# Moving the low halves of the second layer's experts from GpSimd to VectorE, one hidden unit late, in a fused two-layer language-model tower

## The chip, the cores and the metric

The kernel runs on one core of a Trainium2 chip. The metric is the device time of one launch in microseconds (us), the median of several runs. The engines are TensorE (PE, with its weight loads as PEld), VectorE (DVE), ScalarE (ACT), GpSimd (POOL) and SyncE (SP, which issues the DMAs).

## What is computed

4096 tokens (16 rows of 256) pass through two layers of width 256. Cut to what matters here:

```
h = embed(x)
h = h + rwkv_block(layernorm(h))               # layer 0, time and channel mix
h = h + dense_moe(layernorm(h))                # layer 0: 8 experts, hidden 1024, gelu, top-2 gates
h = h + rwkv(layernorm(h))                     # layer 1
x = h; x = x + attention(rms(x))               # layer 1: 16 heads of 16, causal, 256 keys
o0 = gelu(xf @ e0_up.T) @ e0_down.T            # layer 1: four experts on xf = rms(x)
o1 = silu(xf @ e1_w1.T) * (xf @ e1_w2.T) @ e1_down.T
o2 = gelu(gelu(gelu(xf @ e2_l1.T) @ e2_l2.T) @ e2_l3.T) @ e2_l4.T
o3 = gelu(gelu(xf @ e3_down.T) @ e3_up.T) @ e3_out.T
moe = wts0 * o0 + wts1 * o1 + wts2 * o2 + wts3 * o3
```

All products are made from bf16 pairs: a number is kept as a high half (it, rounded to bf16) and a low half (it minus the high half, rounded to bf16), and TensorE adds three products, high by high, high by low and low by high.

## The kernel before, in words

The tokens are cut into 8 tiles of TT = 512. A first phase (to about 457 us) embeds them and runs layer 0's RWKV block. The second phase, `phase_bc`, does the rest, in stages, and each stage works on three tiles at once: the 8 dense experts of layer 0 on tile i, layer 1's RWKV and attention (the `front`) on tile i - 1, and layer 1's four experts on tile i - 2.

**Units.** The work of the experts is cut into units. `U` is an up product of a dense expert with its gelu, `D` the down product of one. `I` is an up product of a second-layer expert with its gelu, `G` the gated one (silu times a product), `O` a down product. `U`, `I` and `G` are the hidden units: each makes one 128 x 512 block of hidden values. A stage has 64 hidden units of the dense experts; a tile of the second layer's experts has 26 (22 `I`, 4 `G`), so 208 for all 8 tiles.

**A hidden unit.** PE fills one of two PSUM banks (`c_up`). ACT takes the gelu into one of four f32 buffers `g` (line 1580) and writes the high half (line 1582); for a `G`, DVE makes the gated value in two steps (`gated`, lines 1934 and 1938) and ACT the high half (line 1572). Then the low half is `g` minus the high half, a `tensor_tensor` of 128 x 512: on DVE for the dense experts (line 1955), on POOL for the second layer's (line 1418). ACT's gelu of hidden unit h waits for the low half of h - 4, since the buffers go round. PE's down products wait for both halves.

**The order.** Nothing is scheduled at run time. Each engine walks the same list of tokens: the front's steps (`f0`, `r2`, `Rb0`, `A1`, `f5d`, `g5`, ...) and, braided between them by fixed weights, the units. Each engine does at a token what is its own there, and waits on semaphores in that order. So an instruction that waits holds up everything behind it on its engine. On POOL the second layer's low halves stand in the same queue as the reciprocal square roots of the norms (lines 1357 to 1380), the low halves of the front's inputs (1386, 1404) and two of every three heads' low halves of the attention weights (1396; DVE does the third at 1851, and the high halves at 1848; ACT the exponentials at 1535). On DVE the dense low half of unit n is already one unit late: it is done at the token of unit n + 1.

**The stages.** One with dense units alone, one with dense units and front, five full ones (`ORDER_BC`, period 313.7 us), one without second-layer units, then `ORDER_CC` (2744 to 3011 us: no dense units, the last front, two tiles of second-layer experts with 52 hidden units) and `PLAN_C` (3011 to 3084 us: the last tile's 26).

Of the kernel before, what the change touches and what calls it, by code (L numbers as in the profile page):

```python
# [8 lines left out]
ALU = mybir.AluOpType  # L9
# [4 lines left out]
BATCH, SEQ, D = 16, 256, 256  # L14
# [779 lines left out]
LAG = 3  # L794
# [97 lines left out]
class Plan:  # L892
# [47 lines left out]
    def braid(self, order):  # L940
# [13 lines left out]
        return tokens + self.units[n:]  # L954

    def last_use(self, piece):

        if piece[0] == "B":
            return self.units.index(("D", 4 * piece[1] + 3))
        users = [n for n, u in enumerate(self.units) if u[0] in "IGO"  # L960
                 and c_piece("e1_w1" if u[0] == "G" else u[1], u[-2]) == piece]
        return users[-1]
# [40 lines left out]
def phase_bc(nc, c, out):  # L1003
# [5 lines left out]
    with ExitStack() as x:  # L1009
# [121 lines left out]
        up_ps = Both(x.enter_context(nc.semaphore("c_up_ps")), NB, len(PLAN_C.bank_user))  # L1131
        hi_ready = Both(x.enter_context(nc.semaphore("c_hi_ready")), NB, len(PLAN_C.hid))
        lo_dense = Both(x.enter_context(nc.semaphore("c_lo_dense")), NB, 0)
        lo_expert = Both(x.enter_context(nc.semaphore("c_lo_expert")), 0, len(PLAN_C.hid))

        def low_half(i, plan, h):

            unit = [u for u in plan.units if u in plan.hid][h]
            if unit[0] == "U":
                return lo_dense.sem, lo_dense.at(i, unit[1] + 1)  # L1140
            return lo_expert.sem, lo_expert.at(i, sum(u[0] != "U" for u in plan.hid if plan.hid[u] <= h))
        g_ready = Both(x.enter_context(nc.semaphore("c_g_ready")), NB, len(PLAN_C.gelu))
# [42 lines left out]
        def slot_of(plan, u):  # L1185

            if u[0] == "U":
                return 8 + u[1] % 6
            return plan.home["e1" if u[0] == "G" else u[1], u[-1]] + u[-2]
# [161 lines left out]
        def _(pool):  # L1351
# [60 lines left out]

            def dense(i, plan, before):
                def step(u):
                    if u[0] in "IG":
                        h, a = plan.hid[u], slot_of(plan, u)
                        pool.wait_ge(hi_ready.sem, hi_ready.at(i, h + 1))
                        pool.tensor_tensor(lo14[:, a, :], g[:, h % 4, :], hi14[:, a, :],  # L1418
                                           ALU.subtract).then_inc(lo_expert.sem, 1)
                return tokens_of(i, plan, step)  # L1420
            run(pool, lambda: None, {}, dense, front, lambda t: {})

        @block.scalar
        def _(act):
# [138 lines left out]
            def dense(i, plan, before):  # L1563
                def step(u):
# [9 lines left out]
                    if h >= 4:  # L1574
                        act.wait_ge(*low_half(i, plan, h - 4))
                    elif before is not None:
                        act.wait_ge(lo_dense.sem, lo_dense.at(i))
                        act.wait_ge(lo_expert.sem, lo_expert.at(i))
                    bias = c.b1[:, u[1]:u[1] + 1] if u[0] == "U" else 0.0
# [13 lines left out]
        def _(dve):  # L1593
# [336 lines left out]
            def dense(i, plan, before):  # L1930
                def gated(u):
                    n, h = plan.up[u], plan.hid[u]
                    dve.wait_ge(gate_th.sem, gate_th.at(first_tile(i), plan.gate[u] + 1))
                    E.done(dve.scalar_tensor_tensor(sl[:, :], sl[:, :], 1.0, ub[n % 2][:, :], ALU.add, ALU.mult))
                    E.settle()
                    dve.wait_ge(up_ps.sem, up_ps.at(i, n + 2))
                    dve.wait_ge(*low_half(i, plan, h - 4))
                    dve.scalar_tensor_tensor(g[:, h % 4, :], sl[:, :], 0.5, ub[(n + 1) % 2][:, :], ALU.mult,
                                             ALU.mult).then_inc(gate_sl.sem, 1)
# [11 lines left out]

                def low(n):
                    h, a = plan.hid["U", n], slot_of(plan, ("U", n))
                    dve.wait_ge(hi_ready.sem, hi_ready.at(i, h + 1))
                    dve.tensor_tensor(lo14[:, a, :], g[:, h % 4, :], hi14[:, a, :],  # L1955
                                      ALU.subtract).then_inc(lo_dense.sem, 1)

                def step(u):
                    if u[0] == "U" and u[1]:
                        low(u[1] - 1)  # L1960
                    if u == ("D", NB - LAG):
                        low(NB - 1)
                    if u[0] == "G":
# [50 lines left out]
        def _(pe):  # L2014
# [220 lines left out]
            def dense(i, plan, before):  # L2235
# [37 lines left out]
                def down(u):  # L2273
                    e, k = divmod(u, HC0)
                    r, o, h, a = ring[u // 4 % 4], u % 4 * CHUNK, plan.hid["U", u], slot_of(plan, ("U", u))
                    pe.wait_ge(hi_ready.sem, hi_ready.at(i, h + 1))
                    pe.wait_ge(*low_half(i, plan, h))
                    for s in range(SUB):
# [22 lines left out]
                def expert_up(name, k, j):  # L2301
# [9 lines left out]
                    else:  # L2311
                        a = plan.home[src, j]
                        xs = (hi14[:, a:a + kc, :], lo14[:, a:a + kc, :])
                        if k == 0:
                            h = plan.hid["I", src, kc - 1, j] + 1
                            pe.wait_ge(hi_ready.sem, hi_ready.at(i, h))
                            pe.wait_ge(*low_half(i, plan, h - 1))
                    n = plan.up["I", name, k, j]
# [11 lines left out]
                def expert_down(name, k, j):  # L2330
# [5 lines left out]
                    pe.wait_ge(hi_ready.sem, hi_ready.at(i, h))  # L2336
                    pe.wait_ge(*low_half(i, plan, h - 1))
                    for s in range(SUB):
# [113 lines left out]
```

## Time and profile before

| | |
|---|---|
| runs (us) | 3082.78, 3074.77, 3085.43; median 3082.78 |
| the profiled execution, its own time | 3086.17 us |
| its span, first to last instruction | 3084.4 us |
| mean granted TensorE clock | 0.969 |
| PE busy | 2768.5 us (90%) |
| DVE busy | 1844.9 us (60%) |
| ACT busy | 1863.6 us (60%) |
| POOL busy | 828.8 us (27%) |
| PE busy, full stages (1401 to 1715 us) | 298.78 of 314 us |
| PE busy, last two stages (2744 to 3084 us) | 213.53 of 267 us and 65.78 of 73 us |

The shares are of the whole span. A row of a group reads: line, engine, operation, output and inputs by the program's names, count, then busy time and mean duration in ns, then the idle time of the engine just before these instructions and what ended most of it.

### The profile page before, as it was taken

The numbers are of one execution on the slowest core, as the hardware profiler recorded it, in microseconds if no ns is written. First come the engines' busy times: TensorE is split into PE (matmuls) and PEld (weight loads), VectorE is DVE, ScalarE is ACT, GpSimd is POOL, SyncE is SP. The second block draws the span as 40 slices with busy tenths as digits, with TensorE's granted clock in tenths as the row PEclk, the third lists the DMA queues.
The fourth block names the chain that finished last, engine by engine and source line by source line (L and its number), as shares of the span: only waits on it lengthen the run. The fifth ranks groups of instructions, "written<-read, shape, count | busy, mean of one in ns | idle before, by whom it ended". The sixth has DMA issues, their size and how long they took to land. (4 is left out here: it accounts for less than half of the span.)

```text
span 3084.4 us, 55991 instructions
## 1 busy us (share of the span) xinstructions
PE 2768.5 (90%) x22208; PEld 1857.4 (60%) x22208; DVE 1844.9 (60%) x3612; ACT 1863.6 (60%) x2899; POOL 828.8 (27%) x846
## 2 busy tenths in 40 slices
PE   3988968998999999999999999999999988997889
PEld 1556545565665667566756675667666756653655
DVE  5776737647657565755566556655665566556452
ACT  3666636556666655666666666666566656765634
POOL 5666520000131222222222222122212211143334
PEclk8999979999999999999999999999999999998999
DMA  1000018721222212221222222212222121210002
GB/s 63 21 27 14 21 35 317 273 103 69 69 95 69 78 59 90 81 90 61 86 84 79 73 70 86 93 64 76 83 85 74 68 76 64 81 34 23 25 23 78
DMA packets 59694, 235.66 MB, mean 76 GB/s; under 512 B 6560, under 2 KB 25024, under 8 KB 40640
## 3 DMA queue, kind: packets, MB, share of 16 engines
q1 hardware_dynamic: 57920, 228.13, 21.3%
q0 software_dynamic: 1536, 4.20, 0.5%
q8 instruction: 169, 2.77, 0.4%
q14 instruction: 69, 0.57, 0.1%
HBM read 200.57 MB, written 31.72 MB: 75 GB/s over the span
## 5 line engine op out<-in xcount | busy, mean ns | idle before, releaser
L2269 PE MATMUL c_up<-c_xT,c_ring 128*128 128x512 bf16 x3072 | 742.2, 381 | 40.9 <-ACT c_g L1580 28.2
L2286 PE MATMUL c_down<-c_ring,c_hi 128*128 128x256 bf16 x4096 | 708.5, 273 | 8.4 <-DVE c_lo L1955 8.2
L1580 ACT ACTIVATE c_g<-c_up,b 128x512 f32<-128x512 f32 x512 | 349.8, 683 | 432.0 <-PE c_up L2269 429.9
L2286 PE MATMUL c_down<-c_ring,c_lo 128*128 128x256 bf16 x2048 | 559.9, 273 | 0.0
L1955 DVE TENSOR_TENSOR c_lo<-c_g,c_hi 128x512 bf16<-128x512 f32 x512 | 372.0, 739 | 209.9 <-ACT c_hi L1582 208.7
L2269 PEld LDWEIGHTS c_up<-c_xT,c_ring 128*128 128x128 bf16 x3072 | 294.9, 98 | 329.8 <-issue 33.2
L1418 POOL TENSOR_TENSOR c_lo<-c_g,c_hi 128x512 bf16<-128x512 f32 x208 | 252.3, 1218 | 819.7 <-ACT c_hi L1582 664.4
L2286 PEld LDWEIGHTS c_down<-c_ring,c_hi 128*128 128x128 bf16 x4096 | 394.6, 98 | 114.7 <-issue 17.7
L1582 ACT ACTIVATE c_hi<-c_g 128x512 bf16<-128x512 f32 x688 | 433.4, 630 | 21.8
L1396 POOL TENSOR_TENSOR c_room<-c_room 128x384 bf16<-128x384 f32 x176 | 189.8, 1091 | 578.3 <-DVE c_room L1848 578.3
L1848 DVE CAST c_room<-c_room 128x384 bf16<-128x384 f32 x256 | 113.9, 469 | 239.7 <-PE c_front L2181 207.8
L1580 ACT ACTIVATE c_g<-c_up 128x512 f32<-128x512 f32 x176 | 104.5, 594 | 248.0 <-PE c_up L2022 245.5
L2286 PEld LDWEIGHTS c_down<-c_ring,c_lo 128*128 128x128 bf16 x2048 | 200.8, 98 | 23.8
L2022 PE MATMUL c_up<-c_hi,c_ring 128*128 128x512 bf16 x712 | 178.5, 389 | 16.4 <-ACT c_g L1580 13.5
L2022 PE MATMUL c_up<-c_yhi,c_ring 128*128 128x512 bf16 x504 | 137.9, 399 | 27.9 <-ACT c_g L1580 25.2
L2342 PE MATMUL c_down<-c_ring,c_hi 128*128 128x192 bf16 x1024 | 142.0, 256 | 14.3 <-DVE h L1949 14.2
L1535 ACT ACTIVATE c_room<-c_front 128x384 f32<-128x384 f32 x256 | 116.0, 489 | 62.0 <-PE c_front L2157 57.9
L1823 DVE TENSOR_REDUCE c_mx<-c_front 128x2 f32<-128x512 f32 (+1 forms) x192 | 117.4, 681 | 42.3 <-PE c_front L2132 37.9
L2153 PE MATMUL c_front<-c_room,c_kz 128*128 128x256 bf16 (+1 forms) x512 | 119.9, 247 | 14.8 <-ACT c_room L1535 14.8
L2342 PE MATMUL c_down<-c_ring,c_lo 128*128 128x192 bf16 x512 | 131.1, 256 | 0.0
L1580 ACT ACT_TABLE_LOAD x101 | 129.6, 1283 | 1.8
L1949 DVE SCALAR_TENSOR_TENSOR h<-c_down,c_gates,h 128x256 f32<-128x256 f32 x256 | 105.9, 475 | 34.8 <-PE c_down L2286 34.8
(339 smaller groups left out, 5280.6 us busy)
## 6 DMA issues: line engine op xcount, KB each, us to landing
c_ring<-kept_dense SPq DMA_DIRECT2D x112, 1024.0 KB, 4.8
c_ring<-kept_experts SPq DMA_DIRECT2D x63, 512.0 KB, 3.3
c_room<-in_WB SPq DMA_DIRECT2D x16, 1024.0 KB, 6.9
kept_dense<-c_ring SPq DMA_DIRECT2D x16, 1024.0 KB, 4.8
c_ring<-kept_experts SPq DMA_DIRECT2D x28, 384.0 KB, 3.4
kept_experts<-c_room SPq DMA_DIRECT2D x9, 512.0 KB, 4.2
c_xT<-kept_xT SPq DMA_DIRECT2D x8, 512.0 KB, 4.5
out<-h SPq DMA_DIRECT2D x8, 512.0 KB, 6.9
```

The costliest lines, as they stand in the source:

```text
L1396: pool.tensor_tensor(pl[:, n % PB, :], pf[:, n % PB, :], ph[:, n % PB, :], ALU.subtract).then_inc(p_lo_pool.sem, 1)
L1418: pool.tensor_tensor(lo14[:, a, :], g[:, h % 4, :], hi14[:, a, :], ALU.subtract).then_inc(lo_expert.sem, 1)
L1535: act.activation(pf[:, n % PB, :], fb[n % 2][:, 0:3 * P], ACT.Exp).then_inc(p_f.sem, 1)
L1580: act.activation(g[:, h % 4, :], ub[n % 2][:, :], ACT.Gelu, bias=bias).then_inc(g_ready.sem, 1)
L1582: act.activation(hi14[:, a, :], g[:, h % 4, :], ACT.Copy).then_inc(hi_ready.sem, 1)
L1823: dve.tensor_reduce(o, fb[n % 4][:, :].rearrange("p (h k) -> p h k", k=w), AX.X, ALU.max).then_inc(mx_ready.sem, 1)
L1955: dve.tensor_tensor(lo14[:, a, :], g[:, h % 4, :], hi14[:, a, :], ALU.subtract).then_inc(lo_dense.sem, 1)
L2022: m = pe.matmul(bank[:, :], w(wp, k, e * P, P), xs[xp][:, k, :], start=(j == 0 and k == 0), stop=(j == 2 and k == kc - 1))
L2153: pe.matmul(bank[:, lo:lo + w], kz[h % 2][:, h // 2, ks_:ks_ + P], qT[:, h // 2, qs_:SEQ], start=True, stop=False, skip_group_check=True)
L2269: last = pe.matmul(ub[n % 2][:, :], r[:, wp, o + q * P:o + (q + 1) * P], xT[:, xp, q, :], start=(m == 0 and q == 0), stop=(m == 2 and q == ...
L2286: m = pe.matmul(bank, (hi14, lo14)[xp][:, a, s * P:(s + 1) * P], r[:, wp, o + KC * P:o + CHUNK], start=False, stop=(k == HC0 - 1 and n == ...
L2342: m = pe.matmul(ob[s // 2][:, (s % 2) * D:(s % 2) * D + DZ], (hi14, lo14)[xp][:, a, s * P:(s + 1) * P], E(plan, wp, name, k, 0, DZ), start ...
```

## The change

POOL does no low halves of hidden units any more. DVE does all of them, by one function `low` with a counter `done`, each at the token of the next hidden unit (and ahead of `gated` where that is a `G`). The last one of a stage comes at a late `D` token, or at an `O` token where the stage has no dense units. One semaphore, `lo_ready`, counts them; there were two. POOL keeps the norms' roots, the inputs' low halves and its two thirds of the attention weights. The instructions on PE and ACT stay the same in kind, number and order. Lines behind line 1418 have other numbers after the change: the low half moves from 1955 to 1946, `gated` from 1934 and 1938 to 1921 and 1925, the cast of attention weights from 1848 to 1835.

```diff
+    def hids_before(self, unit):
+        return sum(u in self.hid for u in self.units[:self.units.index(unit)])
...
-            def dense(i, plan, before):
-                def step(u):
-                    if u[0] in "IG":
-                        h, a = plan.hid[u], slot_of(plan, u)
-                        pool.wait_ge(hi_ready.sem, hi_ready.at(i, h + 1))
-                        pool.tensor_tensor(lo14[:, a, :], g[:, h % 4, :], hi14[:, a, :],
-                                           ALU.subtract).then_inc(lo_expert.sem, 1)
-                return tokens_of(i, plan, step)
-            run(pool, lambda: None, {}, dense, front, lambda t: {})
+            run(pool, lambda: None, {}, lambda i, plan, before: {}, front, lambda t: {})
...
                     if h >= 4:
-                        act.wait_ge(*low_half(i, plan, h - 4))
+                        act.wait_ge(lo_ready.sem, lo_ready.at(i, h - 3))
...
-                def low(n):
-                    h, a = plan.hid["U", n], slot_of(plan, ("U", n))
+                hidden = [u for u in plan.units if u in plan.hid]
+                done = [0]
+
+                def low():
+                    h = done[0]
+                    a = slot_of(plan, hidden[h])
                     dve.wait_ge(hi_ready.sem, hi_ready.at(i, h + 1))
                     dve.tensor_tensor(lo14[:, a, :], g[:, h % 4, :], hi14[:, a, :],
-                                      ALU.subtract).then_inc(lo_dense.sem, 1)
+                                      ALU.subtract).then_inc(lo_ready.sem, 1)
+                    done[0] += 1
 
                 def step(u):
-                    if u[0] == "U" and u[1]:
-                        low(u[1] - 1)
-                    if u == ("D", NB - LAG):
-                        low(NB - 1)
+                    last = ("D", NB - LAG) if plan.dense else u if u[0] == "O" else None
+                    if u in plan.hid and plan.hid[u] > done[0] or u == last and done[0] < plan.hids_before(u):
+                        low()
                     if u[0] == "G":
                         gated(u)
```

On DVE in a full stage, around the third of its four `G` units, which falls among the attention heads: `c_lo` is a low half, `c_room<-c_room` the attention weights, `c_sl` and `c_g` the two steps of `gated`. Before:

```order
L1955 TENSOR_TENSOR c_lo<-c_g,c_hi 128x512 [waits c_hi_ready]
L1848 CAST c_room<-c_room 128x384 [waits c_pv_ps,c_p_f] x2
L1934 SCALAR_TENSOR_TENSOR c_sl<-c_sl,c_up 128x512 [waits c_gate_th]
L1938 SCALAR_TENSOR_TENSOR c_g<-c_sl,c_up 128x512 [waits c_lo_dense,c_up_ps,c_e_steps]
L1848 CAST c_room<-c_room 128x384 [waits c_pv_ps,c_p_f]
```

After the change:

```order
L1946 TENSOR_TENSOR c_lo<-c_g,c_hi 128x512 [waits c_hi_ready]
L1835 CAST c_room<-c_room 128x384 [waits c_pv_ps,c_p_f] x2
L1946 TENSOR_TENSOR c_lo<-c_g,c_hi 128x512 [waits c_hi_ready]
L1921 SCALAR_TENSOR_TENSOR c_sl<-c_sl,c_up 128x512 [waits c_gate_th]
L1925 SCALAR_TENSOR_TENSOR c_g<-c_sl,c_up 128x512 [waits c_lo_ready,c_up_ps,c_e_steps]
L1835 CAST c_room<-c_room 128x384 [waits c_pv_ps,c_p_f]
```

A low half now stands between the two casts and the gated unit.

On POOL in `ORDER_CC`, around the norm ahead of the attention (`c_frs` is the reciprocal root, from the variances `c_fmv` that DVE made; `c_xlo` an input's low half). Before:

```order
L1386 TENSOR_TENSOR c_xlo<-c_room,c_xhi 128x512 [waits c_x_hi] x2
L1418 TENSOR_TENSOR c_lo<-c_g,c_hi 128x512 [waits c_hi_ready] x14
L1376 TENSOR_TENSOR c_frs<-c_fmv,eps 128x4 [waits c_f_var]
L1376 TENSOR_TENSOR c_frs<-c_frs,eps 128x4 [waits c_f_pool]
L1376 TENSOR_TENSOR c_frs<-c_frs 128x4 [waits c_f_pool]
L1376 TENSOR_TENSOR c_frs<-c_frs,c_fmv 128x4 [waits c_f_pool]
```

After the change:

```order
L1382 TENSOR_TENSOR c_xlo<-c_room,c_xhi 128x512 [waits c_x_hi] x2
L1372 TENSOR_TENSOR c_frs<-c_fmv,eps 128x4 [waits c_f_var]
L1372 TENSOR_TENSOR c_frs<-c_frs,eps 128x4 [waits c_f_pool]
L1372 TENSOR_TENSOR c_frs<-c_frs 128x4 [waits c_f_pool]
L1372 TENSOR_TENSOR c_frs<-c_frs,c_fmv 128x4 [waits c_f_pool]
```

The fourteen low halves that stood between the two are gone from POOL's queue. On DVE they come back among its own steps of the front. The rows of DVE after the change, around the division (`RECIPROCAL`) of the front's first half and the first scan of the second half (`c_pp`):

```order
L1722 TENSOR_TENSOR c_room<-c_room 128x512
L1946 TENSOR_TENSOR c_lo<-c_g,c_hi 128x512 [waits c_hi_ready] x2
L1728 RECIPROCAL c_room<-c_room 128x512 [waits c_f_steps]
L1730 SCALAR_TENSOR_TENSOR c_room<-c_room 128x512 [waits c_f_steps]
L1733 SCALAR_TENSOR_TENSOR c_room<-c_room 128x512 [waits c_tr_ready,c_f_steps]
L1946 TENSOR_TENSOR c_lo<-c_g,c_hi 128x512 [waits c_hi_ready]
L1685 SCALAR_TENSOR_TENSOR c_pp<-dec,c_room 128x256 [waits c_kv_ready]
```

Ahead of the division stand two low halves, and one between the first half's output (line 1733) and the second half's scan; before there was none here.

## Rows read from the trace of the kernel before

**Rows 1.** The page: busy time, share of the span, instructions.

```profile
PE 2768.5 (90%) x22208; PEld 1857.4 (60%) x22208; DVE 1844.9 (60%) x3612; ACT 1863.6 (60%) x2899; POOL 828.8 (27%) x846
```

**Rows 2.** The page, costliest groups: the low halves and the attention weights.

```profile
L1955 DVE TENSOR_TENSOR c_lo<-c_g,c_hi 128x512 bf16<-128x512 f32 x512 | 372.0, 739 | 209.9 <-ACT c_hi L1582 208.7
L1418 POOL TENSOR_TENSOR c_lo<-c_g,c_hi 128x512 bf16<-128x512 f32 x208 | 252.3, 1218 | 819.7 <-ACT c_hi L1582 664.4
L1396 POOL TENSOR_TENSOR c_room<-c_room 128x384 bf16<-128x384 f32 x176 | 189.8, 1091 | 578.3 <-DVE c_room L1848 578.3
```

**Rows 3.** Windows: length, then busy time (instructions) of each engine, clock, DMA.

```profile
1401.00:1715.00 314.00, 298.78 (x2475) 202.83 (x2472) 187.57 (x366) 197.82 (x304) 72.40 (x69) 0.99 0.23 79
2744.00:3011.00 267.00, 213.53 (x1764) 135.38 (x1762) 146.24 (x301) 139.22 (x220) 99.95 (x95) 0.92 0.08 24
```

**Rows 4.** Low halves on DVE with POOL all but silent: 560:700, and one pair.

```profile
L1955 DVE TENSOR_TENSOR c_lo<-c_g,c_hi 128x512 bf16<-128x512 f32 x46 | 31.1, 686 | 28.0 <-ACT c_hi L1582 28.0
617.59 1.28 DVE L1955 TENSOR_TENSOR c_lo<-c_g,c_hi 128x512 bf16<-128x512 f32 x2
```

**Rows 5.** Timeline of a full stage, steps `f0` and `r2`: start, duration.

```profile
1551.48 4.63 POOL L1418 TENSOR_TENSOR c_lo<-c_g,c_hi 128x512 bf16<-128x512 f32 x4
1551.55 4.72 DVE L1611 TENSOR_SCALAR c_xn<-h,c_fmv,c_frs 128x256 f32<-128x256 f32 x4 [1.40 <-POOL c_frs L1365]
1554.26 0.22 ACT L1588 ACTIVATE lg<-lg 128x16 f32<-128x16 f32 x1
1556.19 0.16 DVE L1979 TENSOR_REDUCE c_r<-lg 128x4 f32<-128x16 f32 x1
1557.19 1.17 DVE L1991 TENSOR_TENSOR lg<-lg,c_below 128x64 f32<-128x64 f32 x1
1559.25 0.59 ACT L1580 ACTIVATE c_g<-c_up 128x512 f32<-128x512 f32 x1
1562.22 0.69 DVE L1955 TENSOR_TENSOR c_lo<-c_g,c_hi 128x512 bf16<-128x512 f32 x1
```

**Rows 6.** Timeline, the third `G` of a full stage, and PE's stall there.

```profile
1490.03 1.84 POOL L1396 TENSOR_TENSOR c_room<-c_room 128x384 bf16<-128x384 f32 x2 [2.93 <-DVE c_room L1848]
1490.14 0.67 DVE L1934 SCALAR_TENSOR_TENSOR c_sl<-c_sl,c_up 128x512 f32<-128x512 f32 x1
1491.58 0.63 ACT L1572 ACTIVATE c_hi<-c_g 128x512 bf16<-128x512 f32 x1 [3.36 <-DVE c_g L1938]
1494.06 0.28 PE L2153 MATMUL c_front<-c_room,c_kz 128*128 128x256 bf16 x1 [1.25 <-ACT c_room L1535]
```

**Rows 7.** Timeline: a dense low half issued just behind POOL's attention low half.

```profile
1395.40 2.28 POOL L1396 TENSOR_TENSOR c_room<-c_room 128x384 bf16<-128x384 f32 x2 [1.36 <-DVE c_room L1848]
1395.51 1.40 DVE L1955 TENSOR_TENSOR c_lo<-c_g,c_hi 128x512 bf16<-128x512 f32 x1
```

**Rows 8.** Timeline, `ORDER_CC`: a DVE step beside POOL, and one without it.

```profile
2785.00 1.64 DVE L1735 TENSOR_TENSOR c_room<-c_room 128x512 f32<-128x512 f32 x1
2805.80 0.68 DVE L1735 TENSOR_TENSOR c_room<-c_room 128x512 f32<-128x512 f32 x1
```

**Rows 9.** Timeline, `ORDER_CC`: the norm ahead of the attention.

```profile
2820.45 0.37 DVE L1604 BATCH_NORM_AGGREGATE c_fmv<-c_fst 128x2 f32<-128x6 f32 x4
2822.39 1.16 POOL L1418 TENSOR_TENSOR c_lo<-c_g,c_hi 128x512 bf16<-128x512 f32 x1 [11.57 <-ACT c_hi L1582]
2827.02 3.02 DVE L1611 TENSOR_SCALAR c_xn<-h,c_fmv,c_frs 128x256 f32<-128x256 f32 x4 [6.20 <-POOL c_frs L1380]
2829.96 1.37 DVE L1611 TENSOR_SCALAR c_h<-h,c_fmv,c_frs 128x256 f32<-128x256 f32 x4
```

**Rows 10.** Timeline of PE, `ORDER_CC`: its stalls at these steps.

```profile
2812.82 3.60 PE L2044 MATMUL c_front<-c_WF,c_xhi 128*128 128x256 bf16 x16 [4.51 <-ACT c_xhi L1485]
2830.10 1.97 PE L2053 MATMUL c_front<-ident,c_xn 128*128 128x128 f32 x8 [3.89 <-DVE c_xn L1611]
2883.36 0.32 PE L2153 MATMUL c_front<-c_room,c_kz 128*128 128x256 bf16 x1 [1.97 <-ACT c_room L1535]
```

More of the change, by code:

```diff
@@ L1131, in phase_bc @@
         up_ps = Both(x.enter_context(nc.semaphore("c_up_ps")), NB, len(PLAN_C.bank_user))
[L1132 to L1141, printed above, removed]
+        hi_ready, lo_ready = (Both(x.enter_context(nc.semaphore("c_" + n)), NB, len(PLAN_C.hid))
+                              for n in ("hi_ready", "lo_ready"))
         g_ready = Both(x.enter_context(nc.semaphore("c_g_ready")), NB, len(PLAN_C.gelu))
@@ L1574, in step @@
                     if h >= 4:
-                        act.wait_ge(*low_half(i, plan, h - 4))
+                        act.wait_ge(lo_ready.sem, lo_ready.at(i, h - 3))
                     elif before is not None:
-                        act.wait_ge(lo_dense.sem, lo_dense.at(i))
-                        act.wait_ge(lo_expert.sem, lo_expert.at(i))
+                        act.wait_ge(lo_ready.sem, lo_ready.at(i))
                     bias = c.b1[:, u[1]:u[1] + 1] if u[0] == "U" else 0.0
@@ L1936, in gated @@
                     dve.wait_ge(up_ps.sem, up_ps.at(i, n + 2))
-                    dve.wait_ge(*low_half(i, plan, h - 4))
+                    dve.wait_ge(lo_ready.sem, lo_ready.at(i, h - 3))
                     dve.scalar_tensor_tensor(g[:, h % 4, :], sl[:, :], 0.5, ub[(n + 1) % 2][:, :], ALU.mult,
@@ L2276, in down @@
                     pe.wait_ge(hi_ready.sem, hi_ready.at(i, h + 1))
-                    pe.wait_ge(*low_half(i, plan, h))
+                    pe.wait_ge(lo_ready.sem, lo_ready.at(i, h + 1))
                     for s in range(SUB):
@@ L2316, in expert_up @@
                             pe.wait_ge(hi_ready.sem, hi_ready.at(i, h))
-                            pe.wait_ge(*low_half(i, plan, h - 1))
+                            pe.wait_ge(lo_ready.sem, lo_ready.at(i, h))
                     n = plan.up["I", name, k, j]
@@ L2336, in expert_down @@
                     pe.wait_ge(hi_ready.sem, hi_ready.at(i, h))
-                    pe.wait_ge(*low_half(i, plan, h - 1))
+                    pe.wait_ge(lo_ready.sem, lo_ready.at(i, h))
                     for s in range(SUB):
```

## The prediction

> **What bounds the kernel now.** I read the page's busy times first, then the same by stage, then PE's stalls one by one, and last the timelines of DVE and POOL around those that the change can touch. PE is busy 90% of the span, DVE and ACT 60%, POOL 27% [rows 1]. In a full stage PE works 298.78 of 314 us; in ORDER_CC only 213.53 of 267 [rows 3]. So there is little to win in the full stages and, once, some 50 us of stalls in the tail. What counts is not the load of an engine but which wait ends last where PE stands still. A low half is also no bottleneck in itself: POOL's 208 wait 819.7 us in all for what they read [rows 2].
>
> **The work that moves.** POOL loses 208 low halves, 252.3 us at 1218 ns [rows 2]. On DVE one takes 686 ns where POOL is all but silent, and a pair 1.28 us, so one more in a series advances DVE by 0.6 to 0.64 us [rows 4]. Added: 208 x 0.686 = 143 us.
>
> Against it stands what POOL's low halves cost DVE today. Beside four of them, 4.63 us long, the norm's four steps take 4.72 us [rows 5]; the same operation, four times, takes 1.37 us when they are gone [rows 9]. A plain step takes 1.64 us beside POOL and 0.68 without [rows 8]. Both engines' instructions there end together: one waits until the other's is over. Only DVE steps with two SBUF inputs, and the fast one-input ones, show it; the gated unit's, with an input in PSUM, takes 0.67 beside POOL [rows 6]. Going through DVE's steps that overlap a low half of POOL, I estimate some 90 us of such excess over the whole span (an estimate: 0.96 us for each of some 95 blocked steps). DVE's load so rises by about 143 - 90 = 53 us, from 60% to 62%, and it has no work on PE's path by load alone.
>
> The Trainium skill, page "SBUF — State Buffer", section "Who interferes with whom", says that a DVE instruction with two SBUF inputs contends with a GpSimd instruction that reads SBUF, through an exclusive lock held for the whole instruction. The trace agrees (1.64 against 0.68). The rule also speaks against the change: POOL keeps 176 attention low halves, and each new DVE low half has two SBUF inputs, so those that meet will wait for each other.
>
> **Full stages (five).** Of their PE stalls of over half a microsecond, most are ACT's table loads, which stay. Two places were walked.
>
> At f0 and r2 the norm's four steps shrink from 4.72 to about 1.4 and end at 1552.95. Then three low halves, to about 1554.9. The gates' chain (r2) then starts at once, since its exponentials are there from 1554.48 on; today it starts at 1556.19 and ends ahead of the low half at 1562.22, 6.0 us, and POOL's low halves block four of its thirteen small steps, as the one of 1.17 us [rows 5]. Taking 0.8 us off each leaves 2.8 us (an estimate), so it ends at 1557.7. The next low half ends at 1558.4. The gelu that needs it, four units on, starts today at 1559.25 [rows 5]. So nothing is late, with 0.9 us to spare: cost 0. If that cover is gone, ACT's gelus slide by what is missing.
>
> At the third G it costs. Today two casts are followed by the gated unit at 1490.14; its high half starts on ACT at 1491.58, after ACT has idled 3.36 us for it; then ACT loads its table, does the exponentials behind, and PE stands 1.25 us for those [rows 6]. The change puts a low half ahead of the gated unit. ACT's high half for it is long there. At least it costs 0.6 us. But POOL starts an attention low half at 1490.03, 0.11 us ahead. The same offset, 1395.40 and 1395.51, made a dense low half take 1.40 us [rows 7]: then 1.40 less the overlap of 0.07, 1.33. Everything on that path waits for it, and PE at its end. PE shows this stall of 1.24 to 1.51 us in all five stages. Price between 5 x 0.6 = 3.0 and 5 x 1.33 = 6.7; I take 6.5, since the row lies at the same offset. The other three G of a stage have idle time of DVE ahead of or inside them, 0.67 us at the least, and hide a low half of 0.6.
>
> **ORDER_CC, first half (2777 to 2832 us).** No dense units here, so DVE had no low halves and PE waits for DVE. On DVE in the front's first half three steps are blocked (as 2785.00 [rows 8]), -2.9, and two low halves come in ahead of the division, +1.25: the output is 1.65 earlier. The second half's scan: -0.9 and +0.6, so its exponentials come 2.0 earlier. Its own chain: three blocked steps, -2.7, two low halves, +1.25: in all 3.25 to 3.4 us earlier at the stall of 4.51 at 2812.82 [rows 10]. Then the norm. DVE has the variances at 2820.82, but POOL stands in its queue at a low half whose high half ACT makes only at 2822.39, after 11.57 us of idle time; only then come the roots, 3.5 us long, to 2827.0, and the norm's steps, 3.02 us [rows 9]. PE stands from 2826.21 to 2830.10 for the first of them [rows 10]. With POOL's queue free the roots start at 2820.8 less the 3.3 won so far, 2817.5, and end at 2821.0; the norm's steps take 1.4, to 2822.4; PE comes there at 2826.2 - 3.3 = 2822.9. So the stall of 3.89 goes whole. The low half that DVE gets ahead of these steps has its high half in time, and hides beside the roots. Sum: 3.25 + 3.85 = 7.1 us.
>
> **ORDER_CC, second half, and PLAN_C.** The stall of 1.97 at 2883.36 [rows 10] has POOL's attention low half behind a waiting low half in its queue: about -1. Two shorter stalls of that kind follow: another -1 to -1.9. Against these, the 19 low halves that came between attention steps on POOL now stand between DVE's casts and maxima, 0.6 us each, most in its idle time; four or so on a path. I put the half at -2, bounds -4 and +3. PLAN_C's chain does not change but for its last low half, 1.15 to 0.69: -0.5 at most, counted in the -2. Together with the first half: -9, bounds -12 and -4.
>
> **Sum.** 6.5 - 9 = -2.5 us. Against the profiled execution's own 3086.17 this is 3083.7; that execution stands 3.4 us above the median of the runs, so the forecast median is 3082.78 - 2.5 = 3080.3. What a measurement of this kernel can tell from no change is 0.3%, 9.2 us, so this is no change.
>
> **Rivals.**
> (a) Faster: DVE's freedom counts for more. The five third G cost only 3.0 (POOL's attention low half comes elsewhere), the tail gives its full 12: -9; and if each full stage also gives 1 us of those stalls where DVE's blocked steps stand in the chain, -14, 3069. For it: 90 us of blocked time vanish. Against it: in the full stages I find no PE stall that ends at a blocked DVE step.
> (b) Slower: low halves on DVE wait in order for ACT's high halves and for POOL's attention low halves, and the casts of attention weights stand behind them. In ORDER_CC 19 such low halves lie in the attention part. With 1.33 us each on the path, 10 of them are 13.3, and the sum is 6.5 - 7 - 1.5 + 13.3 = +11; from 9 on it decides. With all 19, +23, 3106. For it: POOL idled 11.57 us for one high half [rows 9], and now DVE would. Against it: DVE has 121 of 267 us idle in that stage [rows 3], much of it ahead of its casts, for PE.
> (c) The chain at f0 and r2 ends over 0.9 us later than worked out, and ACT's ring of four g buffers stalls: 1 us more in each of five stages, +2.5, 3085. It stays within 0.3%.
> (d) The full stages' term is hidden after all and the tail gives 7 to 9: 3075, also within.
>
> **How the numbers follow.** Forecast with (c) and (d), within 0.3%: 0.57. (a): 0.25. (b): 0.18. Range: from a little below (a)'s 3069, since (a) can go further than it, to the lower part of (b), which begins at 3092: 3067 to 3094. That leaves out the tail of (a), some 0.06, and most of (b), some 0.13. The forecast's own range is 3074 to 3088.
>
> **What would show it.** In the profile after: POOL about 575 us busy; low halves on DVE x720 near 0.69 to 0.75 us; the norm's steps in f0 at 1.4 us; no stall at f5d's transposes in ORDER_CC, and the two ahead of it 2 and 1 us shorter; the stall behind the third G grown from 1.25 to about 2.5 in five stages. Wrong it would be if that stall has not grown, if DVE's casts in ORDER_CC idle for c_hi, or if ACT's gelus wait for DVE's c_lo.

## The result, and the profile after

| | median (us) | lowest to highest | ratio to before, 95% interval |
|---|---|---|---|
| before | 3082.78 | 3074.77 to 3085.43 | |
| the changed kernel | 3068.41 | 3061.88 to 3073.97 | 0.996 [0.9946, 0.9975] |

The change makes the kernel faster by 0.4%: about 12 us by the ratio of the runs, 14 by the medians. I had forecast 3080.3 and "no change" as the likeliest case. The time lies in the range of 3067 to 3094, but near its end and outside the forecast's own 3074 to 3088: by its size it is the case with a chance of 0.25. In experiments 1 and 9 one run each took far longer than the others (4745.62 and 4037.86 us, at a granted clock of 0.557 and 0.726); their ratios leave these runs out, their medians (3064.37 and 3062.51) count them.

The page of the changed kernel: busy time by engine, then the groups that answer to [rows 1, 2].

```profile
PE 2755.7 (90%) x22208; PEld 1849.9 (60%) x22208; DVE 1891.0 (62%) x3820; ACT 1862.5 (61%) x2899; POOL 583.8 (19%) x638
...
L1946 DVE TENSOR_TENSOR c_lo<-c_g,c_hi 128x512 bf16<-128x512 f32 x720 | 517.6, 736 | 295.0 <-ACT c_hi L1569 290.0
...
L1392 POOL TENSOR_TENSOR c_room<-c_room 128x384 bf16<-128x384 f32 x176 | 193.9, 1113 | 1099.6 <-DVE c_room L1835 1099.6
```

POOL is down from 828.8 to 583.8 us. DVE's busy time grows by 46 us, where 208 low halves at 736 ns would add 153: the rest, 107 us, I take for blocked time that is gone. So far the forecast (53 us more, 62%) holds. PE's busy time, though, falls by 12.8 us with the same 22208 instructions. That is what I had not looked for.

PE runs the same matmuls in the same order in both kernels, so the two traces can be laid side by side matmul by matmul. For each part of the program the table gives the time from its first matmul to the first of the next part, and the sum of PE's gaps in it (time in which no matmul runs), after minus before, worked out from the matmul records of the two traces.

| part (us, before) | time | PE idle |
|---|---|---|
| 0 to 968, no second-layer experts | -3.2 | -1.0 |
| five full stages, 968 to 2537 | +4.1 | +4.0 |
| 2537 to 2744, no second-layer experts | +0.1 | 0.0 |
| ORDER_CC, first part, 2744 to 2850 | -13.1 | -7.6 |
| ORDER_CC, second part, 2850 to 3011 | -5.4 | -0.15 |
| PLAN_C, 3011 to the end | 0.0 | 0.0 |

The first line shows the size of chance between two executions: the program there is the same. The tail (the last two stages, 2744 us to the end) is 18.5 us shorter, but only 7.8 of it is time in which PE stood still. The other 10.7 us is time in which PE was busy, and it goes with the granted clock. Windows over that part of before, with the columns as in [rows 3]; the clock is the third number from the right:

```profile
2744.00:2850.00 106.00, 81.40 (x402) 39.17 (x399) 66.08 (x119) 58.47 (x91) 40.04 (x39) 0.88 0.08 25
2850.00:3011.00 161.00, 132.13 (x1362) 96.21 (x1363) 80.16 (x184) 80.75 (x130) 59.91 (x57) 0.94 0.07 23
```

and the same parts of the changed kernel:

```profile
2744.70:2837.70 93.00, 75.87 (x402) 36.67 (x400) 67.16 (x142) 57.46 (x90) 8.96 (x13) 0.94 0.09 29
2837.70:2993.20 155.50, 126.91 (x1366) 94.41 (x1364) 95.22 (x212) 81.07 (x131) 30.34 (x30) 0.97 0.08 24
```

The same 402 matmul instructions keep PE busy for 81.4 us before and 75.9 after. By the records of the granted clock, PE spends 44.4 us of the tail at 0.5 before and 20.5 us after. Closer, around the norm ahead of the attention, where PE stood 3.89 us [rows 10], before:

```profile
2826.00:2830.00 4.00, 0.20 (x1) 0.00 (x0) 2.98 (x5) 1.23 (x2) 3.17 (x4) 0.86 0.44 131
2830.00:2833.00 3.00, 2.90 (x11) 2.16 (x12) 1.33 (x5) 1.75 (x4) 0.41 (x1) 0.50 0.00 0
2833.00:2837.00 4.00, 4.00 (x14) 1.50 (x13) 0.00 (x0) 1.12 (x3) 1.90 (x2) 0.66 0.00 0
```

and after:

```profile
2820.50:2824.50 4.00, 3.72 (x22) 2.09 (x21) 2.97 (x8) 3.54 (x6) 1.23 (x2) 1.00 0.43 133
2824.50:2828.50 4.00, 3.92 (x24) 2.09 (x23) 1.02 (x3) 2.87 (x6) 1.09 (x1) 1.00 0.00 0
```

Before, PE is granted 0.50 of its clock (1.2 of 2.4 GHz) for 6.8 us in all, from about 1.1 us ahead of the end of the stall on (worked out from the three rows), and in those 3 and 4 us only 11 and 14 matmuls pass; 24 pass in 4 us after the change, where the clock stays at 1.00. Over the tail I count nine stretches at 0.5 before and four after. How much of this the change itself does, and how much is chance between two executions, is a question for experiments 1 and 2.

What happened at the stalls themselves, in the changed kernel: POOL's roots, DVE's steps of the norm, and PE behind them.

```profile
2815.47 0.37 DVE L1591 BATCH_NORM_AGGREGATE c_fmv<-c_fst 128x2 f32<-128x6 f32 x4
2815.92 0.20 POOL L1372 TENSOR_TENSOR c_frs<-c_fmv,eps 128x4 f32<-128x4 f32 x1 [53.06 <-DVE c_fmv L1591]
2819.59 1.38 DVE L1598 TENSOR_SCALAR c_xn<-h,c_fmv,c_frs 128x256 f32<-128x256 f32 x4 [2.01 <-POOL c_frs L1376]
2821.03 1.09 PE L2044 MATMUL c_front<-ident,c_xn 128*128 128x128 f32 x8 [0.28 <-DVE c_xn L1598]
```

The roots start 0.1 us after the variances, not 2.7 us [rows 9], DVE's steps take 1.38 in place of 3.02, and PE waits 0.28 us in place of 3.89. The eight transposes behind take 1.09 us and not 1.97 [rows 10].

Of the stalls ahead of the norm, two have shrunk: one at a product of the second-layer experts, and that of 4.51 us at the front's product [rows 10]. Before, then the two in the changed kernel:

```profile
2792.78 1.89 PE L2022 MATMUL c_up<-c_hi,c_ring 128*128 128x512 bf16 x8 [1.97 <-ACT c_g L1580]
...
2789.93 1.89 PE L2013 MATMUL c_up<-c_hi,c_ring 128*128 128x512 bf16 x8 [0.16 <-ACT c_g L1567]
2808.52 3.52 PE L2035 MATMUL c_front<-c_WF,c_xhi 128*128 128x256 bf16 x16 [3.37 <-ACT c_xhi L1473]
```

Two others there, of 1.49 and 5.48 us before, are 1.49 and 5.18 after.

The full stages lose. The third `G` in the changed kernel, by engine:

```profile
1487.53 2.44 POOL L1392 TENSOR_TENSOR c_room<-c_room 128x384 bf16<-128x384 f32 x2 [2.93 <-DVE c_room L1835]
1487.64 0.68 DVE L1946 TENSOR_TENSOR c_lo<-c_g,c_hi 128x512 bf16<-128x512 f32 x1
1489.68 0.63 ACT L1560 ACTIVATE c_hi<-c_g 128x512 bf16<-128x512 f32 x1 [3.96 <-DVE c_g L1925]
1492.16 0.28 PE L2144 MATMUL c_front<-c_room,c_kz 128*128 128x256 bf16 x1 [1.85 <-ACT c_room L1523]
```

PE's stall grew from 1.25 to 1.85 [rows 6]: by 0.6, the bare low half. So it does in four of the five stages; in the first it grew by 0.3. POOL started 0.11 us ahead, as in [rows 7], but this time POOL was the one that waited (2.44 for two, where it took 1.84), and DVE's low half took 0.68.

And a second place, which I had not seen: the maxima of the attention scores. Before:

```profile
1363.26 4.87 DVE L1823 TENSOR_REDUCE c_mx<-c_front 128x2 f32<-128x512 f32 x8 [2.33 <-PE c_front L2132]
```

After:

```profile
1360.68 0.69 DVE L1946 TENSOR_TENSOR c_lo<-c_g,c_hi 128x512 bf16<-128x512 f32 x1 [3.13 <-ACT c_hi L1569]
1361.29 4.27 DVE L1810 TENSOR_REDUCE c_mx<-c_front 128x2 f32<-128x512 f32 x7
1362.03 0.28 PE L2121 MATMUL c_front<-c_kz,c_room 128*128 128x256 bf16 x1 [0.22 <-DVE c_mx L1810]
```

The two traces are 3.39 us apart there, so the maxima would have started at 1359.87. DVE instead stands 3.13 us, until 1360.68, for a high half from ACT, does the low half, and only then starts on maxima for which PE waits. They are 1.4 us late, and PE, which has to wait for each pair of them, loses 1.2 us in each full stage (0.5 of it as gaps; the rest lies in matmuls that start further apart).

There is a small gain too. At the norm ahead of the attention in each full stage (its transposes start at 1331.43 before), a gap of PE of 0.24 us is gone and the program is 0.4 us earlier behind it: DVE's four steps of that norm take 2.19 us before, beside a low half of POOL, and 1.38 after. Place by place a full stage so loses 0.6 + 1.2 - 0.4 = 1.4 us.

### The profile page after: what moved, and what is told of

Its sections match the earlier page's. It is cut to its first block and busy times, and to the rows that moved or that the text cites. A ratio compares the mean times of both kernels' runs of the same rounds, so it can differ in the third digit from the quotient of the medians.

```text
span 3066.6 us, 55992 instructions
## 1 busy us (share of the span) xinstructions
PE 2755.7 (90%) x22208; PEld 1849.9 (60%) x22208; DVE 1891.0 (62%) x3820; ACT 1862.5 (61%) x2899; POOL 583.8 (19%) x638
## 5 line engine op out<-in xcount | busy, mean ns | idle before, releaser
L1946 DVE TENSOR_TENSOR c_lo<-c_g,c_hi 128x512 bf16<-128x512 f32 x720 | 517.6, 736 | 295.0 <-ACT c_hi L1569 290.0
L1835 DVE CAST c_room<-c_room 128x384 bf16<-128x384 f32 x256 | 95.0, 394 | 223.4 <-PE c_front L2172 195.6
L2013 PE MATMUL c_up<-c_hi,c_ring 128*128 128x512 bf16 x712 | 174.0, 382 | 14.4 <-ACT c_g L1567 11.4
L2013 PEld LDWEIGHTS c_up<-c_hi,c_ring 128*128 128x128 bf16 x712 | 68.3, 98 | 84.4 <-issue 11.6
```

The source lines that it names most:

```text
L2013: m = pe.matmul(bank[:, :], w(wp, k, e * P, P), xs[xp][:, k, :], start=(j == 0 and k == 0), stop=(j == 2 and k == kc - 1))
```

## The experiments

The time of each run stands beside that of the kernel before in the same batch; the two are medians, and the ratio compares all the runs of both, with its 95% interval. Two runs of different batches (1, 2, 3 and 5 are one batch, 4, 6, 7 and 8 another, 9 a third, the changed kernel a fourth) are compared by their ratios to before. PE's idle time by part is worked out as above, against the one trace of before.

**1. VectorE in the tail alone.** Low halves of the full stages stay on POOL. Of the edit, POOL's side; DVE's side does the others, one unit late, as in the changed kernel.

```diff
-                    if u[0] in "IG":
+                    if u[0] in "IG" and plan.dense:
...
```

> Low halves on VectorE only in the last two stages; the full stages are those of before. Theory A (stalls go, and the granted clock of TensorE is back at its upper level there as well): the tail from 2744 us to the end is shorter by about 18 us as in the changed kernel, 7 of it idle time of PE and 11 the clock; the full stages are unchanged; the whole is faster than before by 16 to 19 us, and faster than the changed kernel by some 4. Theory B (the clock's share was chance between two executions): the tail is shorter by 7 to 9 us, PE's idle time by 7, and the whole by 7 to 9.

3064.37 us beside 3079.68, ratio 0.9952 [0.9933, 0.997]. The full stages are those of before within 0.2 us each; the tail is 18.3 us shorter, PE's idle time in it 8.8, and the stretches at half clock are four, as in the changed kernel. The gain is 15 us by the ratio and by the medians, just short of theory A's 16 to 19 and well above the 7 to 9 of theory B, which the interval (9 to 21 us) excludes by little. The 4 us that theory A saw over the changed kernel are 2.5 by the ratios, well inside their intervals. Of the 18.3, the next run shows 3.9 to be within chance.

**2. VectorE in the full stages alone.** The changed kernel, but in the last two stages POOL does its low halves as before. Of the edit, DVE's side:

```diff
...
-                    if u in plan.hid and plan.hid[u] > done[0] or u == last ...
+                    if plan.dense and u in plan.hid and plan.hid[u] > done[0] or plan.dense and u == last ...
```

> Low halves on VectorE only in the five full stages; the last two stages are those of before. Theory A: PE idles 0.85 us more in each full stage (0.6 at the third gated unit and the rest at the maxima of the attention, where a low half waits in order for its high half ahead of them) and the stage is 1.8 us longer apart from the clock: slower by 4 to 9 us. Theory B (freeing VectorE of blocked steps pays in the full stages too): 0 to 3 us faster.

3084.4 us beside 3079.68, ratio 1.0022 [1.0011, 1.0033]: slower. PE idles 3.9 us more in the five stages. The tail is the program of before, all but the same in stalls, with nine stretches at half clock again, yet it is 3.9 us shorter than in the trace of before, 0.6 of it idle time: PE spends 34.1 us of it at 0.5, where it was 44.4. The norm's transposes in it:

```profile
2826.41 1.09 PE L2052 MATMUL c_front<-ident,c_xn 128*128 128x128 f32 x8 [3.89 <-DVE c_xn L1606]
```

The stall is the same 3.89 us, but here the transposes take 1.09 us and not 1.97, since the clock falls only 1 us behind the end of the stall, where in the first trace it fell 1.1 us ahead of it, and for 3.4 us in place of 6.8. So the same stall in the same program is followed by different clocks, and the 1.97 us are no sign of what the change does. The tail in four executions, with the columns as in [rows 3], before, experiment 2, the changed kernel, experiment 1:

```profile
2744.00:3084.40 340.40, 279.31 (x2182) 172.86 (x2179) 163.53 (x343) 172.28 (x274) 129.98 (x121) 0.93 0.11 36
2743.00:3079.50 336.50, 276.03 (x2182) 171.53 (x2179) 165.29 (x343) 172.25 (x274) 130.28 (x121) 0.95 0.12 37
2744.70:3066.60 321.90, 268.59 (x2182) 168.53 (x2179) 195.14 (x421) 171.59 (x274) 39.30 (x43) 0.97 0.12 39
2739.40:3061.50 322.10, 269.82 (x2182) 168.72 (x2180) 195.03 (x421) 171.80 (x274) 39.33 (x43) 0.96 0.12 39
```

Against the two executions of the tail of before, that of experiment 1 is 18.3 and 14.4 us shorter, 8.8 and 8.2 of it idle time; its runs say 15. The part of the clock is what is left: 6 to 10 us.

**3. The queue alone.** The kernel before, but in the last two stages POOL does its low halves one hidden unit late. Its reads stay.

```diff
...
+                    elif (u in plan.hid and plan.hid[u] > done[0]
+                          or u[0] == "O" and done[0] < plan.hids_before(u)):
+                        low_of(done[0])
+                        done[0] += 1
```

> The kernel before, but in the last two stages GpSimd does its low halves one hidden unit late: its queue holds nothing ahead of the norm any more, while its reads beside VectorE stay. Theory A with the queue as the larger part: PE's stall of 3.89 us at the transposes behind the norm shrinks by 2 to 3 us, and those of 1.97 and 5.48 and 4.51 stay; idle time of PE in the tail falls by 2 to 3.5 us, the clock gives 2 to 5 more: faster by 4 to 8 us. Theory B (blocked VectorE steps are the whole of it): no stall changes by over 0.5 us, and the time by less than 2.

3069.94 us beside 3079.68, ratio 0.9974 [0.9964, 0.9984]: 8 to 10 us faster without any change to DVE. POOL and PE at the norm:

```profile
2813.86 0.20 POOL L1380 TENSOR_TENSOR c_frs<-c_fmv,eps 128x4 f32<-128x4 f32 x1 [8.67 <-DVE c_fmv L1619]
...
2820.45 1.09 PE L2068 MATMUL c_front<-ident,c_xn 128*128 128x128 f32 x8 [1.76 <-DVE c_xn L1626]
```

POOL is now free when the variances come, and the stall is 1.76 in place of 3.89, with the transposes behind it at the upper level (1.09 us). The stalls of 1.49, 1.97 (at 2792.78) and 5.48 stay. Stalls at the attention products go too: PE's idle time falls by 2.2 us between 2880 and 2910, where the stall of 1.97 at 2883.36 [rows 10] is down to 0.95, and by 4.3 us in the whole second part of ORDER_CC. Theory B is excluded. Theory A had the kind and the time about right, but not the idle time: that falls by 7.3 us in the tail and not by 2 to 3.5, since the queue of POOL had also held up its low halves of the attention weights (PE's waits for these in the tail fall from 3.3 to 1.0 us). The order of POOL's queue alone gives 8 to 10 of the tail's 15 us.

```profile
2739.30:3068.20 328.90, 275.12 (x2182) 171.54 (x2179) 166.64 (x343) 172.21 (x274) 130.34 (x121) 0.95 0.12 38
```

Laid beside the four executions above, this one says something about the clock. Its idle time, 328.90 - 275.12 = 53.8 us, is all but that of the changed kernel, 53.3; yet it is 7 us longer, and spends 34.1 us at 0.5 where the changed kernel spends 20.5. Against experiment 2 it has 6.7 us less idle time and is 7.6 us shorter. So by these traces a removed stall was worth about its length here (1.1 to 1.4 times by the 8 to 10 us of the runs), and in experiment 1 nearly twice that.

**4. POOL's reads put back.** The changed kernel; in the tail POOL makes a subtraction of the same shape on other data, one unit late. Its result is not used; each also waits for the one before it.

```diff
...
+                    pool.wait_ge(hi_ready.sem, hi_ready.at(i, done[0] + 1))
...
+                    pool.tensor_tensor(xT[:, 1, 1, :], xT[:, 0, :, :]....bitcast(F32), xT[:, 1, 0, :], ALU.subtract)
```

> The changed kernel; in the last two stages GpSimd makes in addition a subtraction of the same shape on other data, from the same waits, one hidden unit late, whose result nobody uses. Theory A (half of the tail's gain is VectorE's freedom from GpSimd's reads, the rest the queue ahead of the norm): the steps of the recurrence are blocked again, PE's stalls of 1.49/1.97/5.48 are back within 0.5 us of before or longer, the queue's part of some 8 us stays; slower than the changed kernel by 5 to 9 us. Theory B (the queue alone): within 2 us of the changed kernel.

3093.78 us beside 3080.77, ratio 1.0044 [1.0031, 1.0057]: some 26 us slower than the changed kernel by the ratios, against 5 to 9 expected. DVE over the tail, its low halves and one of the steps of the recurrence:

```profile
L1966 DVE TENSOR_TENSOR c_lo<-c_g,c_hi 128x512 bf16<-128x512 f32 x79 | 72.0, 932 | 35.3 <-ACT c_hi L1589 31.7 <-ACT c_hi L1580 3.5
...
2789.26 1.65 DVE L1738 TENSOR_TENSOR c_room<-c_room 128x512 f32<-128x512 f32 x1
```

In the changed kernel the same low halves take 705 ns:

```profile
L1946 DVE TENSOR_TENSOR c_lo<-c_g,c_hi 128x512 bf16<-128x512 f32 x78 | 54.1, 705 | 44.4 <-ACT c_hi L1569 40.6 <-ACT c_hi L1560 3.5
```

The steps of the recurrence (layer 1's RWKV) are back at 1.65 us, and the low halves are blocked as well, since both engines are released by the same high half. In the trace the tail is 21.7 us longer than in the changed kernel, 12.8 of it idle time of PE. Theory A's mechanism is shown; its size was too low, for I had counted only the steps that were blocked before, not the low halves themselves. POOL's queue is longer in this kernel too, but experiment 3 had the same queue and was faster than before, so the queue alone is not the cause. That the stalls come back "within 0.5 us" did not hold singly: that of 0.16 in the changed kernel is 4.01 (1.97 before), that of 5.18 is 3.61 (5.48 before). The Trainium skill's page "SBUF — State Buffer", section "Who interferes with whom", states this lock between a VectorE instruction with two SBUF inputs and a GpSimd one that reads; the trace agrees, 932 ns against 705.

**5. and 6. The wait ahead of the norm put back.** The changed kernel, and one wait of POOL ahead of the roots, first for the high half of before, then for that of the next hidden unit.

```diff
+                    if isinstance(t, int) and t == TILES - 1:
+                        h = PLAN_CC.hid["I", "e2_l3", 3, 0]      # then ("I", "e2_l3", 0, 1)
+                        pool.wait_ge(hi_ready.sem, hi_ready.at(TILES, h + 1))
+                    both_norms()
```

> The changed kernel, with one wait more: ahead of the norm of the last front GpSimd waits for the high half that its queue had to wait for before the change. It does no low half there. Theory A: PE's stall at the transposes behind the norm is back with 1.5 to 3.5 us, and the granted clock falls behind it for some 4 us, another 2 to 3: slower than the changed kernel by 3.5 to 6.5 us, faster than before by 8 to 11. Theory B (the blocked steps alone gave the time): within 1 us of the changed kernel.

3068.91 us beside 3079.68, ratio 0.9967 [0.9954, 0.998]. PE's stall there is back by 1.4 us only (1.64 in place of 0.28), just under the 1.5 to 3.5 of theory A. The whole is 2 us slower than the changed kernel by the ratios, 4 by the medians, and the intervals of some 4 us to either side leave both theories open. That the wait is short has a likely reason, which no run tests: the stalls ahead of the norm are shorter now, so the high half that POOL waits for also comes earlier.

> As the kernel with one wait put back ahead of the norm, but for the high half of the next hidden unit, some 2.6 us later. Theory A (a stall of PE that is long enough costs its own length and a stretch at the lower granted clock behind it): PE idles 2 to 2.6 us more there than with the first wait, and the stretch behind is at the lower level for some 4 us, as before the change, which costs 2 to 3 more; slower than the changed kernel by 4 to 7 us. Theory B (the clock does not hang on this stall): slower by the idle time alone, 3 to 4 us, with the clock at its upper level behind it.

3076.33 us beside 3080.77, ratio 0.9985 [0.9976, 0.9994], some 8 us slower than the changed kernel. The stall and the transposes behind it:

```profile
2824.65 1.09 PE L2050 MATMUL c_front<-ident,c_xn 128*128 128x128 f32 x8 [3.74 <-DVE c_xn L1604]
```

The stall is 3.74 us, nearly the 3.89 of before, yet the transposes take 1.09 us, at the upper level; in the windows behind the granted clock is 0.5 from about 2826 on, for some 3 us. That part of the program is 4.9 us longer than in the changed kernel, 3.4 of it idle time, so 1.5 us went by the clock. The 8 us exceed both theories, and the comparison of a single trace leaves it open whether the stall costs more than its length: the clock behind it is that of experiment 2, where the same 3.89 us of the kernel before were followed by 3.4 us at 0.5, and not that of the first trace of before, where it was 6.8.

**7. Two low halves moved in the full stages.** The changed kernel; the one ahead of the maxima goes to the next hidden unit, and at the third `G` it comes behind the gated value.

```diff
...
+                    if plan.dense and u == ("G", 2, 0):
+                        gated(u)
+                    if plan.dense and u == ("I", "e3_down", 0, 0):
+                        return
-                    if u in plan.hid and ...
+                    while u in plan.hid and ...
                         low()
-                    if u[0] == "G":
+                    if u[0] == "G" and not (plan.dense and u == ("G", 2, 0)):
                         gated(u)
```

> The changed kernel with two low halves of each full stage moved: the one ahead of the attention's first maxima goes behind them, to the next hidden unit, and at the third gated unit the low half comes behind the gated value. Theory A (these two places are the whole loss of the full stages): PE's idle time in a full stage is back at that of before within 0.1 us, 0.85 less than in the changed kernel, each of the two places is back, and the time is 3 to 5 us below the changed kernel, level with the kernel that has the tail alone on VectorE. Theory B (VectorE's higher load costs at other places too): under 1.5 us below the changed kernel.

3061.16 us beside 3080.77, ratio 0.9942 [0.9927, 0.9956], the fastest of all with the first run of experiment 9. The stall behind the third `G`, and the maxima:

```profile
1356.76 4.87 DVE L1810 TENSOR_REDUCE c_mx<-c_front 128x2 f32<-128x512 f32 x8 [2.33 <-PE c_front L2127]
...
1487.57 0.28 PE L2148 MATMUL c_front<-c_room,c_kz 128*128 128x256 bf16 x1 [1.25 <-ACT c_room L1523]
```

Both are as before the change to the hundredth: 2.33 us of waiting for PE ahead of the maxima, and 1.25 us of stall [rows 6]. PE's idle time in the five stages is 0.6 us below that of before in all, and the time is 5.5 us below the changed kernel by the ratios, a little above the 3 to 5 expected. So these two places were the whole loss; the small gain at the norm, 0.24 us of a gap in each stage, stays. Theory A is shown.

**8. Two low halves moved in the tail.** Experiment 1 with the low halves ahead of the second half's maxima and first `G` moved behind them.

```diff
...
+                    held = plan is PLAN_CC and u in (("I", "e3_up", 3, 1), ("G", 0, 0))
```

> The low halves on VectorE in the last two stages alone, and two of them there moved from ahead of the second half's maxima and first gated unit to behind it. Theory A: the stall that grew there by some 0.6 us and the one after it by 0.4 shrink back; 0.5 to 2 us below the kernel with the tail alone, 15 to 18 below before. Theory B: the moved ones delay the next gated unit, and nothing is won.

3063.71 us beside 3080.77, ratio 0.9955 [0.9942, 0.9968], the same as experiment 1 (0.9952) within the intervals. PE's idle time in the tail is 0.3 us below that of experiment 1: some of it went at one place and came back at another. No gain can be told.

**9. POOL's attention low halves on DVE too,** on top of experiment 7: in the last front, then in all eight.

```diff
...
-                            if n % HEADS % 3 == 2:
+                            if n % HEADS % 3 == 2 or (isinstance(t, int) and t == TILES - 1):    # then: or True
...
```

This is POOL's side, which leaves them out; DVE makes them under the same condition.

> The kernel with two low halves moved, and in the last front GpSimd makes no low halves of attention weights either: VectorE makes all 32. Theory A (GpSimd's reads still cost VectorE time on PE's path in the last front's attention): 22 more operations of some 0.56 us on VectorE, less what its blocked casts lose; the two small stalls of PE at attention products shrink; 1 to 4 us below the kernel with the two moved. Theory B (what is left of the blocking lies in idle time): within 2 us of it, or slower by up to 5, since a cast and its low half now follow each other on one engine.

3062.51 us beside 3078.43, ratio 0.994 [0.9927, 0.9954]: no difference to experiment 7 (0.9942). Theory A's gain of 1 to 4 us is not seen, though the intervals could hide its lower part; it looks as if what is left of the blocking lies in idle time, as theory B has it.

> The same in all eight fronts: VectorE makes all 256 low halves of the attention weights, 176 more at about 0.56 us, 97 us of work; its share rises to 63 or 65%. Theory A (VectorE gets its blocked time back and PE does not wait for it): within 3 us of the kernel with the two moved. Theory B (in the full stages VectorE works on PE's path at the attention, as at the maxima, and each addition there is paid): 3 to 15 us slower than it.

3067.52 us beside 3078.43, ratio 0.9969 [0.9957, 0.9981]: some 8 us slower than experiment 7 by the ratios, as theory B has it (3 to 15). The division of the attention weights between the two engines is worth keeping. These two traces miss some 300 matmul records, so they were not laid beside the others.

## Why the prediction came out as it did

**DVE's load** (143 us more, 90 less, 62%): right in kind. Measured +46 us, 62%.

**f0 and r2, cost 0:** right. The norm's steps take 1.38 us and the chain runs from 1552.76 to 1555.58, 2.8 us as estimated. The low half behind it is done at about 1556.2; the gelu that needs it starts at 1557.35, as early against the matmuls around it as before. Spare: 1.1 us, where I had 0.9.

```profile
1549.65 1.38 DVE L1598 TENSOR_SCALAR c_xn<-h,c_fmv,c_frs 128x256 f32<-128x256 f32 x4 [1.40 <-POOL c_frs L1361]
1550.95 1.89 DVE L1946 TENSOR_TENSOR c_lo<-c_g,c_hi 128x512 bf16<-128x512 f32 x3
1552.76 0.16 DVE L1970 TENSOR_REDUCE c_r<-lg 128x4 f32<-128x16 f32 x1
1555.58 2.58 DVE L1946 TENSOR_TENSOR c_lo<-c_g,c_hi 128x512 bf16<-128x512 f32 x4
...
1557.35 0.59 ACT L1567 ACTIVATE c_g<-c_up 128x512 f32<-128x512 f32 x1
```

**The third `G`, 5 x 1.33 = 6.7:** the place was right, the size not. It cost four times 0.6 and once 0.3, 2.7 in all, about the lower bound. I chose the upper one because a row showed the same offset; but the offset does not say which engine is blocked, and here it was POOL.

**The rest of the full stages, nothing:** wrong. The low half ahead of the maxima costs 1.2 us a stage, 6 in all; the norm ahead of the attention gives back 0.4 a stage, 2 in all, of which I had also seen nothing. It is the mechanism of rival (b), a low half that waits in order for its high half with DVE's work for PE behind it, but I had looked for it in ORDER_CC only. That the term of 6.5 for the full stages comes out about right is luck: 2.7 + 6 - 2 = 6.7 place by place, 4.1 in the trace with its clock, and 4.7 by the medians or 6.8 by the ratio in experiment 2.

**ORDER_CC's first half, 7.1 us of stalls:** right, 7.6 measured: 3.6 at the norm, where I had 3.85, and 1.8, 0.3 and 1.1 at the three stalls ahead of it, where I had 3.25; the rest, 0.7, is a small stall at the end of this part that I had not in the sum. Queue and blocked steps both count, as argued; experiments 3 and 4 show each by itself.

**The second half, -2, bounds -4 and +3:** in idle time -0.15, but in time -5.4, outside the bounds. This is not the chance of one trace: in experiment 2, whose second half is the program of before, that part is within 0.1 us of before. The stalls there only moved: 1.97 is down to 0.95 at 2883.36 [rows 10], others have grown.

**The sum is where it failed:** each stall of PE entered with its own length, and the granted clock with nothing. The tail's 8 us of stalls came with 6 to 10 us of clock, 15 in all where I had 9. I had the clock of 0.92 in ORDER_CC in front of me [rows 3], and 0.99 in the full stages, and did not ask what it would do when the stalls change. The two parts measured alone, -15 (experiment 1) and +5 to +7 (experiment 2), add to -8 to -11; the changed kernel has -12, with an interval of -17 to -8. That the time lies in the range at all is owed to rival (a), whose 3069 set its lower end, and (a) was right for another reason: the full stages did not gain, and the tail's stalls gave 8, not 12. The stall behind the third `G`, which I had named as a sign, grew, but to 1.85 and not to 2.5.

Open is what decides where the clock falls. The same stall of 3.89 us in the same program was followed by 6.8 us at 0.5 in one execution and 3.4 in another. The clock's gain also does not go by the sum of the stalls: experiment 3 removes nearly as much idle time as the changed kernel and wins little more than half as much, and most of what the change wins by the clock beyond chance, some 5 of 7 us, lies in the second half of ORDER_CC, where the sum of the stalls is the same. What is shown is the gain over the tail as a whole.

## What to carry to other kernels

Where TensorE's granted clock is below its upper level in a stretch, the forecast of a change there needs a term for the clock, with wide bounds: here stalls that went were worth from 1.1 to nearly 2 times their length, and no run shows a rule for it. A single trace of before is not enough to read that term; a second execution of the same stretch, here that of experiment 2, shows how much is chance. In a program whose engines walk a fixed order, look for every place at which the moved instruction stands ahead of work that PE waits for, and ask of each whether what it reads is there by then; list those places from the order, for all stages, not only where the engine is known to be short. Two small moves then gave back what the change had cost.

## What was not expected of the hardware

Of two instructions that start 0.11 us apart on POOL and DVE, sometimes the one and sometimes the other is blocked: DVE's took 1.40 us [rows 7] in one place and 0.68 in another, where POOL's pair grew from 1.84 to 2.44. And two executions of one and the same program part differ by up to 6.4 us in 968 (before and experiment 7, from the start to 968), with the granted clock's falls at different places.
